# Turning the probabilities of unit w-2 ahead of the scores of unit w

## What is computed

```python
q_c = hidden_size @ Wq_c.T + bq_c
q = (q_c @ Wq_up.T + bq_up).reshape(b, s, NH, Q_HEAD).transpose(0, 2, 1, 3)
kv = hidden_size @ Wkv_c.T + bkv_c
...
scores = jnp.einsum('bhqd,bhkd->bhqk', q, k) / np.sqrt(Q_HEAD)
attn = jax.nn.softmax(scores, axis=-1)
o = jnp.einsum('bhqk,bhkv->bhqv', attn, v)
out = jnp.einsum('bhsv,Hv->bsH', o, Wo) + bo
```

## Time and profile before

| | |
|---|---|
| median of three runs | 2293.58 us (2293.39 to 2295.8) |
| the profiled execution | 2297.99 us, its span 2296.2 us |
| mean granted clock of PE | 0.971 |
| PE busy, share of the span | 95% |
| PEld, DVE, ACT, POOL | 75%, 70%, 51%, 31% |
| attention, steady part | 22.58 us for a pair of heads (eight units) |

### The profile page before, as it was taken

The page is one execution under the profiler, slowest core; times in us unless marked ns, Lnnn a source line. Parts: engine busy times, 40 slices in busy tenths (PEclk is TensorE's granted clock), DMA queues, the critical chain, the costliest instruction groups (busy, mean ns, idle before and its releaser), DMA issues.

```text
span 2296.2 us, 35305 instructions
## 1 busy us (share of the span) xinstructions
PE 2180.8 (95%) x14449; PEld 1717.9 (75%) x14452; DVE 1602.0 (70%) x1702; ACT 1169.1 (51%) x1757; POOL 703.6 (31%) x330
## 2 busy tenths in 40 slices
PE   6799999999999999999999999996799889999998
PEld 5577888888888788788888878885487657777764
DVE  6668777777777877777777777776722437777765
ACT  3455554554455455554455545542633247777761
POOL 2143333343335333343334333434244200000001
PEclk8899999999999999999999999997899889999999
DMA  2111111111111111111111111101032210000000
GB/s 90 40 49 37 35 36 36 40 39 48 30 39 48 30 39 39 39 39 39 39 30 48 39 38 29 47 22 29 19 92 92 57 48 16 23 16 24 17 2 37
DMA packets 43551, 89.37 MB, mean 39 GB/s; under 512 B 13952, under 2 KB 23040, under 8 KB 43264
## 3 DMA queue, kind: packets, MB, share of 16 engines
q1 hardware_dynamic: 43392, 87.12, 12.9%
HBM read 83.82 MB, written 3.28 MB: 38 GB/s over the span
## 4 chain that ended last, share of the span: by engine, by line
PE 84%; DVE 9%; ACT 3%; issue 2%; POOL 1%; DMA 1%; SPq 0%; ACTq 0%; DVEq 0%
PE PS L538 19%; PE PS L539 17%; PE PS L540 17%; PE PS L609 5%; PE PS L774 3%; PE PS L858 3%; PE PS L578 2%; PE PS L843 2%; PE PS L605 2%; PE PS L585 2%; PE PS L532 2%; PE PS L865 1%; PE PS L832 1%; PE PS L834 1%; PE PS L833 1%
## 5 line engine op out<-in xcount | busy, mean ns | idle before, releaser
L538 PE MATMUL PS<-xnh,wh 128*128 128x512 f32 x1272 | 511.7, 402 | 10.6 <-DVE xnl L1316 5.8
L540 PE MATMUL PS<-xnh,wl 128*128 128x512 f32 x1272 | 498.4, 392 | 0.0
L539 PE MATMUL PS<-xnl,wh 128*128 128x512 f32 x1272 | 498.2, 392 | 0.0
L1362 DVE SCALAR_TENSOR_TENSOR arena<-PS,arena 128x1020 f32<-128x1020 f32 (+2 forms) x240 | 305.0, 1271 | 45.0 <-ACT arena L1039 36.2
L405 POOL TENSOR_TENSOR arena<-arena 128x1024 f32<-128x1024 f32 x64 | 173.3, 2708 | 428.1 <-ACT arena L1018 428.1
L538 PEld LDWEIGHTS PS<-xnh,wh 128*128 128x128 f32 x1272 | 240.1, 189 | 69.6 <-issue 6.6
L540 PEld LDWEIGHTS PS<-xnh,wl 128*128 128x128 f32 x1272 | 240.2, 189 | 51.4
L539 PEld LDWEIGHTS PS<-xnl,wh 128*128 128x128 f32 x1272 | 240.4, 189 | 46.5
L400 POOL TENSOR_TENSOR wl<-arena,wh 128x1024 fp32r<-128x1024 f32 x72 | 175.0, 2430 | 256.8 <-ACT wh L1001 256.8
L1006 ACT ACTIVATE PS<-PS 128x1024 f32<-128x1024 f32 x128 | 129.2, 1009 | 234.3 <-PE PS L578 234.3
L409 POOL TENSOR_TENSOR zl<-arena,zh 128x1024 fp32r<-128x1024 f32 x63 | 150.0, 2381 | 295.8 <-ACT zh L1022 295.8
(11 more groups left out here) (225 smaller groups left out, 4198.2 us busy)
## 6 DMA issues: line engine op xcount, KB each, us to landing
arena<-in_w_xg SPq DMA_DIRECT2D x72, 512.0 KB, 3.6
arena<-in_w_o SPq DMA_DIRECT2D x32, 512.0 KB, 3.6
arena<-in_w_f SPq DMA_DIRECT2D x28, 512.0 KB, 3.6
arena<-in_w_h SPq DMA_DIRECT2D x16, 257.0 KB
arena<-scr SPq DMA_DIRECT2D x256, 6.0 KB
x<-in_x SPq DMA_DIRECT2D x2, 1024.0 KB, 8.3
arena<-scr SPq DMA_DIRECT2D x128, 3.0 KB
out<-x SPq DMA_DIRECT2D x8, 256.0 KB, 2.0
```

Source lines behind the costliest of these rows:

```text
L538: mm(PS[:, bank], ah, bh, start=(n == 0), stop=False)
L539: mm(PS[:, bank], ah, bl, start=False, stop=False)
L540: last = mm(PS[:, bank], al, bh, start=False, stop=(n == len(terms) - 1))
L1362: ins = stt(o, pair_of(bank).rearrange("p q (b t) -> p q b t", t=SEQ)[:, :, :, :SEQ - k], w[:, 3 - k:4 - k], o, ALU.mult, ALU.add)
```

## The change

In PE's loop over the units the call of `turn_p(w - 2)` moves from behind `scores(w)` to ahead of it. The four transposes of the unit two steps back, with the waits that stand in `turn_p`, now come before the six score matmuls of the new unit and their waits. Nothing is added or removed, and the loops of the other engines and SP's DMAs are as before. For w = 0 and 1 there is nothing to turn, and for w = 128 and 129 there are no scores, so the order differs for w = 2 to 127.

```diff
             for w in range(NV + 5):
                 i, v = divmod(w, 2 * NB)
+                if 2 <= w < NV + 2:
+                    turn_p(w - 2)
                 if w < NV:
                     scores(w)
-                if 2 <= w < NV + 2:
-                    turn_p(w - 2)
                 if w % 2 == 0 and 4 <= w < NV + 4:
                     values(w // 2 - 2, i, v)
```

## The result

The changed kernel took 2349.66 us (median of 4 runs, 2347.69 to 2350.02) beside 2294.69 us for the kernel before (2293.39 to 2297.07): a ratio of 1.0237, 95% interval 1.0219 to 1.0254, so 55 us slower (50 to 58). The forecast was 2351, +57.1, with a range of 2333 to 2372.

What follows compares the result with a forecast made beforehand. PE was taken to bound the kernel, with a DVE path hidden until the change. Terms of +1.0, +5.0, +40.1, +4.1 and +6.9 gave +57.1 on the 2293.6 us median: 2351 us, range 2333 to 2372.

Steps and rivals of the forecast that it cites:

- The cover: PE work between the end of scores(w-1) and turn_p(w-2): smallest 2.17 us before; after, 1.40 odd, 1.01 at v = 6.
- path of 1.75: DVE's row maximum, scaling, reciprocal and normalisation, from the end of scores(w-1) to PE's transposes: 1.75 us without POOL's collision.
- the loop: Transposes wait for DVE, scores stand behind them, and DVE's next row maximum needs those scores: one turn per step.
- v = 2: Step of the eight in a head pair with values and fold: 3.21 us, 0.20 of it for the first matmul after values.
- DVE-bound step: Five of a pair's eight steps, where PE waits for DVE: 1.75 + 0.66 + 0.72 = 3.13 us.
- step with `sum_up`: Steps v = 0 and 4 of a pair, where PE is the later one: 2.07 + 0.44 + 0.72 = 3.23 us.
- unknown transition from transposes to scores: New boundary on PE, in no row of before: taken as nothing, with +25 us as the upper end.
- POOL: Subtraction L469 holds DVE's L1543, 14 times: 0.6 us each, 8.4 us taken, bounds 0 to 13 us.
- rival 1: DVE wins the port race, so L1543 ends before POOL starts: 2342 us, chance 0.15.
- No change: Weight loads busy only 77% of the stage, so PE's 23% of slack absorbs the wait: 2294 us, chance 0.02.
- Faster: Probabilities ready when turn_p comes, so the 8.2 us wait and 12.6 us at values go: 2273 us, chance 0.03.
- Clock: PE idles in most steps and the granted clock falls to 1.2 GHz for the stage: 2570 us, chance 0.03.

Runs made afterwards that it cites:

- e1: Changed kernel with DVE's order turned round, norm(w-1) ahead of top(w): 2305.43 us, ratio 1.0047.
- e5: Kernel before with the row maximum L1542 issued twice: 2312.31 us, ratio 1.0075.
- e6: Changed kernel with the row maximum L1542 issued twice: 2437.05 us, ratio 1.0618.
- e7: Changed kernel with DVE's normalisation L1548 on the first half of the columns alone: 2327.93 us, ratio 1.0144.
- e2: Changed kernel with the transposes ahead of the scores in even steps alone, odd steps as before: 2315.85 us, ratio 1.0090.
- e8: Changed kernel with POOL's subtraction L469 on one element: 2344.70 us, ratio 1.0214.
- e4: Kernel before with transposes behind values in even steps, and ACT's copy behind its exponentials and values copy: 2284.27 us, ratio 0.9954.

## Why the prediction was right

**The cover.** Named as 1.40 in odd steps and 1.01 at v = 6 against a path of 1.75. e1 cuts the path's dependence on the scores, e5 and e6 lengthen it in both orders, e7 shortens it: each moved the time by what the loop asks, and the rivals that put the cost on PE are out. The comparison itself was too generous by 0.22 us (e2). In the kernel before the smallest cover, 2.17, was above 1.97 all the same, and after the change the steps below the path stay the same five and v = 2 comes level, so it cost the prediction nothing; with a smallest cover between 1.75 and 1.97 it would have.

**The step.** Forecast 3.13 for a DVE-bound step, 3.15 measured; 3.23 for the step with `sum_up`, 3.22 measured. For v = 2 3.21 was forecast, with 0.20 for the first matmul behind values. In truth the transposes stand there, at 0.59 instead of 0.44, and DVE's path is about as late: 3.15. PE is what bounds this step: with the path 0.26 us shorter (e7) it still takes 3.15 (2021.04 to 2024.19). The unknown transition from transposes to scores was taken as nothing and is nothing: the first score matmul takes 0.12 at 2003.72.

**POOL.** 0.6 taken, 3.68 - 3.15 = 0.53 measured by the step and 0.53 by e8. The prediction counts 14 holds; L1543 is held fully in 13 pairs. The forecast that POOL would come earlier relative to L1543 and hold it for less than before (0.71 against 1.09) was right; rival 1 (DVE first) did not happen.

**The sum.** Twelve full pairs: 12 x (25.85 - 22.58) = +39.2, forecast 40.1. The whole attention: +56.2 in the profiled executions, forecast 57.1; by the medians +55.0. Counted between the row maxima L1542 of the same units, each term holds by itself: +1.1 up to w = 2 (forecast 1.0), +4.7 to w = 11 (5.0), +39.2 to w = 107, +4.1 to w = 115 (4.1) and +7.0 to w = 127 (6.9). So the total is not a sum of large errors that cancel; inside the pair, five steps 0.02 longer and small overestimates at v = 2 and for POOL do cancel.

**The rivals.** No change: PE had no room, though its weight loads were busy only 77% of the stage. The measure of the Trainium skill (Perfetto Trace Analysis, Identifying the Most-Contended Engine), by which the 23% would be headroom, would have given 2294; in e4 the chain of a full pair has no wait of PE left, and the pair is still 22.01 us. Faster: it needed a path under 1.01 us; e7 shortened the path to about 1.49 and was still 1.4% slower than before. Its price was too high as well: 0.20 was counted as won at each `values`, but transposes that stand there pay 0.15 of it themselves, so 0.05 is left (e4). Clock: 1.00 in the changed kernel from 1872 us to the end of the attention (both kernels enter it at 0.50, up to the first units). With the idle time of this order, and with more of it (e6, PE busy 303 of 400 us from 1925 to 2325), it held for the stage; in e5 to e8 it fell for a few microseconds at the end, at a price of a few microseconds where it was read (e8).

## What to carry to other kernels

Before moving a waiting instruction ahead in an engine's order, find what the producer has queued ahead of the value: the probabilities were two steps old, but their last operation stood behind one that needed the newest scores. Compare the length of that path with the work that is left as cover in each kind of step, and add the part that a streaming engine loads ahead (0.22 us here). A full engine gains by an order that lengthens its cover where another engine can be held: here the opposite move took 10 us off, 0.34 us of a pair by the hidden hold and 0.23 by cheaper transitions between matmuls.

## What was not expected of the hardware

- What a group of matmuls takes depended on what stood before it. Behind values (eight matmuls of 64 columns of weights): 0.20 more for scores (0.32 against 0.12) and for `sum_up` (1.06 against 0.86), 0.15 more for transposes (0.59 against 0.44). Behind transposes: nothing.
- The granted clock was 1.00 with PE busy 3.75 of 8 us in one execution, and fell to 1.2 GHz for some 6 us behind a stretch of 3.92 of 8 us in another kernel's.
- A small operation of DVE (L1543, 128x2 elements, 0.17 us) took 0.71 and 1.09 us where a subtraction of POOL (1.29 us) lay over it. What that costs hangs on the order of a third engine: 0.53 us a pair in the changed kernel, 0.34 in the one before, nothing in e4.
